# A feed-forward that decodes its 4-bit weights four blocks ahead of their use, where it was six

## The reference

```python
def dequant4(codes, absmax):
    w = NF4[codes].reshape(o, i // BLOCK, BLOCK) * absmax[:, :, None]
    ...
y1 = x1 @ Wg + x1 @ g_lora_a @ g_lora_b
y2 = x1 @ Wu + x1 @ u_lora_a @ u_lora_b
x3 = jax.nn.relu(y1) * y2
y3 = x3 @ Wd + x3 @ d_lora_a @ d_lora_b
```

## Time and profile before

| | before |
|---|---|
| median of three runs | 2270.62 us |
| lowest and highest | 2267.35, 2271.98 us |
| the profiled execution | 2267.95 us |
| its span, first to last instruction | 2266.2 us |
| mean granted TensorE clock | 0.981 |

### The profile page before, as it was taken

How to read it: one execution, slowest core, us unless ns; L and a number is a source line. 1 busy time by engine, 2 the same in 40 slices (tenths; PEclk the granted TensorE clock), 3 DMA queues, 4 the chain that set the end, 5 groups by cost and what they waited for, 6 DMA issues and landing times. The chain is left out here.

```text
span 2266.2 us, 26427 instructions
## 1 busy us (share of the span) xinstructions
PE 2153.9 (95%) x10082; PEld 1076.0 (47%) x10082; DVE 1112.2 (49%) x2047; ACT 1157.1 (51%) x1823; POOL 424.3 (19%) x444
## 2 busy tenths in 40 slices
PE   7882999999999999999999999999799999988999
PEld 6761444444444444444444444444355555544444
DVE  6883242442525252432525252434577777756443
ACT  5667656656565665656565665653233343324111
POOL 1111211112121211112121211211132223321000
PEclk9995999999999999999999999999999999999999
DMA  5433111121111111111111111111200000000111
GB/s 191 165 116 110 52 56 53 47 62 47 52 56 47 56 53 52 51 57 47 56 52 54 55 47 53 56 47 66 93 19 19 19 19 19 19 0 1 50 50 50
DMA packets 55374, 125.52 MB, mean 55 GB/s; under 512 B 8336, under 2 KB 8720, under 8 KB 55120
## 3 DMA queue, kind: packets, MB, share of 16 engines
q1 hardware_dynamic: 55248, 123.84, 16.6%
HBM read 115.42 MB, written 8.39 MB: 55 GB/s over the span
## 5 line engine op out<-in xcount | busy, mean ns | idle before, releaser
L614 ACT ACTIVATE level<-level 128x512 f32<-128x512 f32 x924 | 581.8, 630 | 29.3
L791 PE MATMUL ps_ring<-xT_hi,gu_hi 128*128 128x512 f16 x1376 | 522.5, 380 | 2.0 <-DVE rel L718 2.0
L791 PE MATMUL ps_ring<-xT_lo,gu_hi 128*128 128x512 f16 x1376 | 522.2, 380 | 0.0
L791 PE MATMUL ps_ring<-xT_hi,gu_lo 128*128 128x512 f16 x1376 | 522.1, 379 | 0.0
L707 DVE SCALAR_TENSOR_TENSOR wt<-level,w_scale,absm 128x512 f32<-128x512 f32 x132 | 98.8, 748 | 496.0 <-ACT level L614 496.0
L726 DVE SCALAR_TENSOR_TENSOR X<-ps_ring,ffn_gain,X 128x512 f32<-128x512 f32 x352 | 260.1, 748 | 145.1 <-PE ps_ring L812 145.1
L812 PE MATMUL ps_ring<-dn_hi,hid_hi 128*128 128x512 f16 x704 | 266.9, 379 | 0.0
L812 PE MATMUL ps_ring<-dn_hi,hid_lo 128*128 128x512 f16 x704 | 266.8, 379 | 0.0
L812 PE MATMUL ps_ring<-dn_lo,hid_hi 128*128 128x512 f16 x704 | 266.7, 379 | 0.0
L668 POOL TENSOR_TENSOR gu_lo<-wt,gu_hi 128x512 f16<-128x512 f32 x88 | 102.7, 1167 | 766.7 <-ACT gu_hi L620 766.7
L791 PEld LDWEIGHTS ps_ring<-xT_hi,gu_lo 128*128 128x128 f16 x1376 | 134.6, 98 | 163.2 <-issue 1.1
(11 more groups left out here) (200 smaller groups left out, 2828.5 us busy)
## 6 DMA issues: line engine op xcount, KB each, us to landing
codes<-in_codes SPq DMA_DIRECT2D x132, 256.0 KB, 2.8
absm<-in_absmax SPq DMA_DIRECT2D x264, 128.0 KB, 3.0
X<-in_x SPq DMA_DIRECT2D x16, 512.0 KB, 4.1
c_in<-in_ctx SPq DMA_DIRECT2D x16, 512.0 KB, 5.1
cT<-in_ctxT SPq DMA_DIRECT2D x16, 512.0 KB, 3.5
xT_hi<-in_ctx SPq DMA_DIRECT2D x8, 1024.0 KB, 4.8
out<-X SPq DMA_DIRECT2D x16, 512.0 KB, 2.6
w<-in_w SPq DMA_DIRECT2D x1, 4096.0 KB, 14.4
```

The costliest lines, as they stand in the source:

```text
L614: act.activation(level[u % 2][:], codes[u % RING][:] if k == 0 else level[u % 2][:], ACT.Prelu, bias=bias, scale=scale, alpha=alpha).then_ ...
L791: mm = pe.matmul(o[:], w[c][:, m, k, :], xx[:, k, ts], start=(q == 0), stop=(q == 3 * KD - 1))
```

## The change

One constant of `phase_nf4_ffn` is changed. Slot k treats unit 4 + k instead of 6 + k, four units instead of six are decoded ahead of the first slot, and `lora_parts` for the next pair stands in slot 7 instead of slot 5. In the last pair units 4 to 11 are treated in slots 0 to 7, instead of units 6 to 11 in slots 0 to 5.

```diff
@@ -489,7 +489,7 @@
     RING = 3
     ACC_FIRST = 8
     HID_FIRST = 2
-    AHEAD = 6
+    AHEAD = 4
     UPS = 2 * TB
     SLOTS = UNITS
     PER_SLOT = 2 * TILES // (SLOTS - UPS)
```

## The result

The changed kernel takes 2301.25 us (median of four, 2301.02 to 2303.14) against 2269.39 us for the kernel before beside it: a ratio of 1.0145, 95% interval 1.0132 to 1.0157, some 32 us more. 2305 us was forecast, with a range from 2293 to 2317.

What follows compares the result with a forecast made beforehand. TensorE was taken to bound the feed-forward stage, so only its gaps matter: -11.3 + 24 + 12.4 + 2.2 + 8.5 = +35.8 us on 2267.95 gives 2303.7, or 2306.4 with the median's 2.7 us; predicted 2305 us, range 2293 to 2317.

Steps and rivals of the forecast that it cites:

- The start, -11.3 us: Before pair 0: four units decoded instead of six bring the first dense matmul to 207.78; -11.3 us (-11.3 to -10).
- Slots 0 and 4, nothing: Units needed in slots 0 and 4 are still ready in time, with 2.8 us or more to spare: 0 us.
- Slot 8, +24 us: First down matmul waits for unit 11, now decoded in slot 7: 2.4 us in ten pairs, +24 us (23 to 26).
- rival 3: Slots 7/8 border: unit 11 already finished, only the start's gain left, 2256.7 us; rivals 3 and 4 together 0.05, half faster.
- The last pair, +12.4 us: Units 8 to 11 fall into short slots at ScalarE's 8.27 us pace, delaying down: +12.4 us (10 to 14).
- The restart, +2.2 us: After the last pair's 12 us gap TensorE restarts at 1.2 GHz: +2.2 us (1.7 to 3.4).
- The dips, +8.5 us: Half of the ten slot 8 gaps followed by a clock dip costing 1.7 us: +8.5 us (0 to +17).
- The case without dips: Rival 1: no clock dips after the ten slot 8 gaps; sum +27.3 us, 2295 to 2298 us; chance 0.22.
- The rule of the Trainium skill: Warns against idle gaps longer than slot 8's; by it alone the dip term is 0 and the rise about 27 us.

Runs made afterwards that it cites:

- five ahead: Changed kernel with the constant AHEAD at 5 instead of 4: 2268.74 us, ratio 0.9998.
- the wait alone: Kernel before, with the first down block of the first ten pairs also waiting for slot 7's unit, which it does not need: 2297.82 us, ratio 1.0124.
- the one with the rounding first: Changed kernel, with ScalarE rounding unit 11 ahead of the relu in slot 7 only: 2284.13 us, ratio 1.0062.
- the last pair alone: Kernel before, with units 6 to 11 decoded two slots later, in slots 2 to 7, in the last pair only: 2283.55 us, ratio 1.0061.
- the gaps filled: Changed kernel, with TensorE running ten matmuls of overwritten result in each of the ten gaps: 2296.48 us, ratio 1.0120.

## Why the prediction held

- **The start, -11.3 us.** First dense matmul forecast at 207.78, measured at 207.76. The border of slots 7 and 8 stands 11.25 us earlier (294.52 against 305.77), so 0.1 us of the gain was lost in the first pair. No up product waited; the clock was at 1.2 GHz for 4.68 us from the first dense matmul, where it was 4.47 us before, and half of the difference is 0.1 us. Right.
- **Slots 0 and 4, nothing.** No wait of the up product for a low half. Right; five ahead and the wait alone say the same.
- **Slot 8, +24 us.** 2.39 us a pair, 23.9 us. The subtraction's release took 0.06 us against the 0.05 assumed. Right in size. The step on its cause was incomplete: it read the relu ahead of the rounding as what made the unit late, and rival 3 held that the rounding ahead of the relu would close the gap. The experiment closed only 1.34 of 2.21 us. The prediction had moved the LoRA preparation to slot 7 at no cost, with ScalarE's idle time as its cover; that idle time lies ahead of the relu, and it covers nothing once the unit itself is what the next slot waits for. As long as the relu stood in front, this was hidden, so the sum did not suffer.
- **The last pair, +12.4 us.** The pace of 8.27 us a unit read from two rows held for the two units more: unit 11 starts to decode at 1578.03 and the down block follows at 1586.89, 8.86 us later, where 8.85 us were worked out. 12.47 us measured, 14.4 us with its restart when made alone. The restart, +2.2 us: right, and luck has a part in how exactly. From the last pair's first down matmul to the next stage it was 43.01 us before and 45.24 us in the changed kernel, but 44.48 us in the kernel with the last pair alone and 45.88 us in the one with the rounding first: a restart of 1.5 to 2.9 us.
- **The dips, +8.5 us.** This term was too large: three dips of ten, 5.0 us. It was given as half of the gaps because one row went each way. 0.17 x 10 / 0.5 = 3.4 us a dip and 1.65 us of cost were right. With 5 in place of 8.5, and the 1.2 us by which the later stages came out longer, the sum of 35.8 becomes 33.5, and 33.4 is what the spans differ by. By the medians the rise is 32 us. The forecast of 2305 us also held part of the 2.7 us by which the median stood above the profiled execution before; in the changed kernel the two are the same (2301.25 and 2301.36), so this part and the dips made it too high, and the 1.2 us took a little of that back.
- **The rivals.** The case without dips had 2295 to 2298 us and was missed by its three dips; with the gaps filled it is what was measured, 2296.48 us. The rule of the Trainium skill ("TensorE: Matmul & The Clock Gate", section "Why this matters for your kernels"), by which none of the ten gaps would lower the clock, was right for seven of them here and eight of ten in the kernel with the wait alone.

## What to carry to other kernels

The depth of a prefetch has two ends: each block less in front brings the first use nearer by one block's time, once, and in the full pairs here nothing was lost until the last block of a group was finished in the slot just before its use; then what its chain reaches past the slot's end was paid at every group. Look for that border in the timeline of the deeper version, where the chain is already there with nobody waiting, and list all that stands in it, in every queue: taking out the foremost cause uncovers the next. And where a stage's end is shorter per slot than its middle, work it out by itself, and let the depth grow from a small start rather than pick one constant.

## What the hardware showed beyond that

Equal gaps did not have equal effects on the clock. Of twenty gaps of 2.21 us amid dense matmuls in two kernels, five were followed by 3.4 us at 1.2 GHz; of ten gaps of 0.87 us none, and of ten filled ones none. The idle time was needed, but at this length it did not bring a dip every time. What picks the five was not settled: the gaps, the work around them and the distance between them were the same.
